# The first product of a chained matmul kernel in another order: high-by-high products first, then those with low parts

## The reference

```
x = x + einsum('bct,bcd->bdt', x, W0[cond0])        # 64 x 64 mixers of the rows
x = x + einsum('bct,bcd->bdt', x, W1[cond1])
x = x + x @ W.T + (x @ lora_A[i]) @ lora_B.T * 0.5   # 1024 x 1024, low rank 32
x = x + x @ W3[adapter].T                            # one of 8 matrices a batch
```

## Time and profile before

| | us |
|---|---|
| median of 3 runs | 394.82 |
| lowest and highest | 394.56, 395.0 |
| the profiled execution | 394.66 |
| its span, first to last instruction | 392.9 |

### The profile page before, as it was taken

The page is one execution under the profiler, slowest core; times in us unless marked ns, Lnnn a source line. Parts: engine busy times, 40 slices in busy tenths (PEclk is TensorE's granted clock), DMA queues, the critical chain, the costliest instruction groups (busy, mean ns, idle before and its releaser), DMA issues.

```text
span 392.9 us, 7604 instructions
## 1 busy us (share of the span) xinstructions
PE 380.2 (97%) x1736; PEld 316.4 (81%) x1736; DVE 268.3 (68%) x285; ACT 231.2 (59%) x307; POOL 123.3 (31%) x163
## 2 busy tenths in 40 slices
PE   8999999999999999999999999899999999999990
PEld 8888888888888888888888887688888888888860
DVE  4746967865855958547967439953699546899563
ACT  3798859387232775244483549554677357777361
POOL 0000340100003000024865427763258434576400
PEclk9999999999999999999999999999999999999996
DMA  7984902740348475406526224742276322762223
GB/s 225 396 313 158 375 3 79 261 180 19 107 173 288 182 277 166 180 21 214 175 93 221 58 55 123 260 133 55 56 235 211 97 57 56 270 219 54 56 58 88
DMA packets 24219, 61.37 MB, mean 156 GB/s; under 512 B 1938, under 2 KB 2066, under 8 KB 24146
## 3 DMA queue, kind: packets, MB, share of 16 engines
q1 hardware_dynamic: 23808, 60.30, 46.1%
q10 hardware_dynamic: 338, 0.24, 0.2%
HBM read 52.15 MB, written 8.39 MB: 154 GB/s over the span
## 4 chain that ended last, share of the span: by engine, by line
PE 96%; issue 1%; DVE 1%; ACT 0%; POOL 0%; ACTq 0%; DVEq 0%; POOLq 0%
PE ps L1400 44%; PE ps L1286 13%; PE ps L1287 13%; PE ps L1288 13%; PE ps L1427 4%; PE ps L1313 4%; PE ps L1325 2%; PE ps L1257 1%; PE ps L1265 1%; DVE stage L1236 0%; DVE stage L1177 0%; ACT stage L706 0%; DVE aT L1214 0%; PE ps L1446 0%; ACT stage L798 0%
## 5 line engine op out<-in xcount | busy, mean ns | idle before, releaser
L1400 PE MATMUL ps<-ring,aT 128*128 x784 | 180.8, 389 | 0.0
L1400 PEld LDWEIGHTS ps<-ring,aT 128*128 128x128 f32 x784 | 147.1, 188 | 30.8 <-issue 0.4
L1286 PE MATMUL ps<-ring 128*128 128x512 f32 x224 | 88.3, 394 | 0.0
L1287 PE MATMUL ps<-ring 128*128 128x512 f32 x224 | 88.0, 393 | 0.0
L1288 PE MATMUL ps<-ring 128*128 128x512 f32 x224 | 87.9, 392 | 0.0
L429 POOL TENSOR_TENSOR aT<-xT,aT 128x512 fp32r<-128x512 f32 (+1 forms) x36 | 56.3, 1585 | 51.3 <-ACT aT L685 45.2
L1149 DVE TENSOR_TENSOR ring<-raw,ring 128x1024 f32 (+1 forms) x40 | 63.8, 1655 | 5.1 <-ACT ring L671 5.0
L694 ACT ACTIVATE aT<-ps 64x1024 fp32r<-64x1024 f32 x32 | 32.7, 1021 | 48.1 <-PE ps L1400 47.6
L1177 DVE TENSOR_TENSOR stage<-ps,stage 64x1024 f32<-64x1024 f32 x30 | 36.7, 1222 | 26.3 <-ACT stage L706 25.7
L1166 DVE TENSOR_TENSOR aT<-ps,aT 64x1024 fp32r<-64x1024 f32 x32 | 39.1, 1222 | 22.6 <-ACT aT L694 21.9
L1288 PEld LDWEIGHTS ps<-ring 128*128 128x128 f32 x224 | 42.6, 190 | 9.0
(11 more groups left out here) (82 smaller groups left out, 314.5 us busy)
## 6 DMA issues: line engine op xcount, KB each, us to landing
raw<-w3t SPq DMA_DIRECT2D x40, 512.0 KB, 4.4
ring_f<-xt SPq DMA_DIRECT2D x8, 1024.0 KB, 7.7
raw<-xt SPq DMA_DIRECT2D x8, 1024.0 KB, 5.1
out<-stage SPq DMA_DIRECT2D x30, 256.0 KB, 3.0
ring_f<-wt SPq DMA_DIRECT2D x4, 1024.0 KB, 7.4
xT<-xt SPq DMA_DIRECT2D x3, 1024.0 KB, 9.5
xT<-wt SPq DMA_DIRECT2D x2, 1024.0 KB, 15.2
ring_f<-xt SPq DMA_DIRECT2D x4, 256.0 KB, 6.4
```

Source lines behind the costliest of these rows:

```text
L1286: pe.matmul(dst, hi_of(qw)[:, k, cs], hi_of(qx)[:, k, :], start=start and k == 0, stop=False, skip_group_check=True)
L1287: pe.matmul(dst, hi_of(qw)[:, k, cs], lo_of(qx)[:, k, :], start=False, stop=False, skip_group_check=True)
L1400: last = pe.matmul(acc(i)[:, n, :], x3_split(i, k, start, P), ring[:, bass.ds(off + (part * D + n * 512), 512)], start=(k == 0 and j == 0) ...
```

## The change

Four things are done:

1. SP issues W's tile ahead of x's tile, for each `k`.
2. ACT takes W's tile before x's. For `k` = 0, columns 128 to 511 of W, which the identity doesn't touch, are rounded as soon as the tile has landed (new semaphore `w_hi_off`), then x's tile, then W's first 128 columns after `A11`. For `k` = 1 to 3 it waits for `A11`, makes `w_hi`, then `x_hi`.
3. PE takes, for each `k`, the four high-by-high matmuls (one to each bank; for `k` = 0 in the order `o` = 1, 2, 3, 0), then the four with `x_lo`, then the four with `w_lo`. Each group of four waits for just its parts.
4. The events that tell of a finished bank are then on the last four matmuls of the product.

DVE's order is unchanged. The count of matmuls is unchanged (48).

```diff
@@ SP
             for k in range(HALF):
                 one = slice(k, k + 1)
+                sp.dma_start(raw_of(w_slot(0))[:, one, :], w_block(1, 1)[:, one, :]).then_inc(s(f"w_in0_{k}"), 16)
                 sp.dma_start(raw_of(x_slot(0))[:, one, :], x_block(1, 0)[:, one, :]).then_inc(s(f"x_in0_{k}"), 16)
-                sp.dma_start(raw_of(w_slot(0))[:, one, :], w_block(1, 1)[:, one, :]).then_inc(s(f"w_in0_{k}"), 16)
@@ ACT
-            for k in range(HALF):
+            act.wait_ge(s("w_in0_0"), 16)
+            act.activation(hi_of(w_slot(0))[:, 0, P:], raw_of(w_slot(0))[:, 0, P:], ACT.Copy).then_inc(s("w_hi_off"), 1)
+            act.wait_ge(s("x_in0_0"), 16)
+            x_hi(0, raw_of(x_slot(0)), slice(0, 1))
+            act.wait_ge(s("A11"), 1)
+            act.activation(hi_of(w_slot(0))[:, 0, 0:P], raw_of(w_slot(0))[:, 0, 0:P], ACT.Copy).then_inc(s("w_hi"), 1)
+            for k in range(1, HALF):
                 one = slice(k, k + 1)
+                act.wait_ge(s("A11"), k + 1)
+                w_hi(0, raw_of(w_slot(0)), one)
                 act.wait_ge(s(f"x_in0_{k}"), 16)
                 x_hi(0, raw_of(x_slot(0)), one)
-                act.wait_ge(s("A11"), k + 1)
-                w_hi(0, raw_of(w_slot(0)), one)
@@ PE
+            w, x = (hi_of(w_slot(0)), lo_of(w_slot(0))), (hi_of(x_slot(0)), lo_of(x_slot(0)))
             for k in range(HALF):
-                for o in range(HALF):
-                    last = main(0, 0, ps_l2(0, 0, o), o, True, True, (k,))
-                    if k == HALF - 1:
-                        last.then_inc(s("l2"), 1)
+                for a, b in ((0, 0), (0, 1), (1, 0)):
+                    high = (a, b) == (0, 0)
+                    if high and k == 0:
+                        pe.wait_ge(s("w_hi_off"), 1)
+                        pe.wait_ge(s("x_hi"), 1)
+                    elif high:
+                        pe.wait_ge(s("w_hi"), k + 1)
+                        pe.wait_ge(s("x_hi"), k + 1)
+                    elif b:
+                        pe.wait_ge(s("x_lo"), k + 1)
+                    else:
+                        pe.wait_ge(s("w_lo"), k + 1)
+                    for o in (1, 2, 3, 0) if high and k == 0 else range(HALF):
+                        if high and k == 0 and o == 0:
+                            pe.wait_ge(s("w_hi"), 1)
+                        last = pe.matmul(ps_l2(0, 0, o), w[a][:, k, P * o:P * (o + 1)], x[b][:, k, :],
+                                         start=high and k == 0, stop=k == HALF - 1 and a == 1, skip_group_check=True)
+                        if k == HALF - 1 and a:
+                            last.then_inc(s("l2"), 1)
```

More of the change, by code:

```diff
@@ L1281, in main @@
                     if whole_wait:
-                        whole = 1 if w == 0 and n == 0 else 2
-                        pe.wait_ge(s("w_lo"), HALF * w + (k // whole + 1) * whole)
-                        pe.wait_ge(s("x_lo"), HALF * n + (k // whole + 1) * whole)
+                        pe.wait_ge(s("w_lo"), HALF * w + (k // 2 + 1) * 2)
+                        pe.wait_ge(s("x_lo"), HALF * n + (k // 2 + 1) * 2)
                     cs = slice(P * o, P * (o + 1))
```

## The result

The changed kernel takes 396.21 us (median of 9 runs, 395.24 to 397.52) against 394.37 us of the kernel before (9 runs, 393.38 to 395.0). The ratio is 1.005, with a 95% interval of 1.0034 to 1.0066: slower by 1.3 to 2.6 us. The profiled execution took 396.93 us with a span of 395.2.

What follows compares the result with a forecast made beforehand. PE was taken to bound the kernel, holding 96% of the chain of waits. The median 394.82 us, plus 0 on PE (from -0.16) and 0 to 0.2 of stall, gave 394.9, own range 394.5 to 395.1, wider range 394.3 to 395.6.

Steps and rivals of the forecast that it cites:

- Worth 0: Head of the first product: PE arrives at 9.53, after low parts (9.06) and high parts (8.0), so its change gains 0.
- a sign that the forecast is wrong: PE's first 23 us: any idling of PE there would show the forecast wrong.
- The line of identity, high parts, low parts: Tiles 1 to 3 on ACT and DVE: steps run one after another, 2.75 us a tile; mixers' copy starts at 16.28.
- DVE's `a_tab` part would end at 22.19, as ACT reaches the selection at 22.24, so it adds nothing: Ahead of the first selection: waiting for `a_tab` adds 0 to ACT's lateness of 0.6 us, or 0.8 without overlap.
- The room at the first delta: `low_split` was done at 36.52, weights loaded at 37.26: room of 0.74 us before lateness of ACT stalls PE.
- the second place: Second low-rank products: x block 3 done at 48.27, weights loaded at 49.05, so 0.78 us of room.
- Rival 1: ACT and DVE steps don't overlap: ACT 1.9 us late, PE stalls at the first delta, 396.1 us; chance 0.09 in full.
- Rival 2: Head of the first product: PE did wait there unseen, and the new order gains, giving 394.5 us; chance 0.09.
- Rival 3: First product: the clock changes level at another moment; chance 0.03 for a gain, 0.02 for a loss.
- 392.6: Gain case of Rival 3: clock rises at the product's start, eleven matmuls run faster, 2.2 us gained; chance 0.03.
- 402 us: Loss case of Rival 3: alternating banks keep the clock low to the product's end, 7.2 us lost; chance 0.02.

Runs made afterwards that it cites:

- pe_only: The kernel before with only PE's new order (first four high-by-high products wait for all of `w_hi` of tile 0): 394.16 us, ratio 0.9993.
- act_only: The kernel before with only ACT's and SP's part of the change, PE keeping its old order: 395.99 us, ratio to before 1.0039.
- regs_after: The changed kernel with ACT reading the eight labels of the first four selections into registers early: 394.35 us, ratio to before 0.9992.
- regs_before: The kernel before with eight labels read early, four ahead of the first tile and four behind the mixers' copy: 394.5 us, ratio 0.9998.
- delay_one: The kernel before with one more ACT copy between x block 2 and the first selection: 394.45 us, ratio 1.0.
- delay3: The kernel before with three more ACT copies between x block 2 and the first selection: 397.72 us, ratio 1.0083.
- pool_b: The kernel before with PE's new order, early label reads, `b_split` and `b_diff` copies on GpSimd, DVE's part of them earlier: 394.76 us, ratio 1.0013.

## Why the prediction was wrong, point by point

- **PE's part, right in the sum and wrong in its reason.** "Worth 0" holds: `pe_only` is at 0.9993. But not because PE comes late to the product's head. I read from one profile that PE begins at 9.53 with the low parts long ready. In all eleven other profiles with the warm-up the mixer products take 2 to 2.6 us instead of 3.68, and end between 7.4 and 8.5, before the low parts are ready. There the new order does start the product earlier: at 8.53, against 9.90 in `act_only`, which has the same order on ACT and SP. The wait is also shorter (1.08 us against 2.02), the level held after it, and PE reaches the next product at 20.06 against 23.77. This lead goes into the waits up to the first delta, because `low_split` comes no earlier (38.59 against 38.71). PE idled ahead of 8.53 and again ahead of 20.06, in the first 23 us, which I had named as a sign that the forecast is wrong.
- **The line of identity, high parts, low parts: right.** 2.75 us for a tile were forecast and 2.72 measured; the mixers' copy was to start at 16.28 and started at 16.55, x block 2 at 20.33 and 20.58. The late landing of x's first tile (ACT starts on it at 7.75, where 7.38 was forecast) covers that difference of 0.25.
- **"DVE's `a_tab` part would end at 22.19, as ACT reaches the selection at 22.24, so it adds nothing": the step that failed.** The two times were nearly right (22.45 and 22.59), the conclusion wasn't. Ahead of a selection stands not only ACT but its sequencer, and that waits for `a_tab` first and reads labels then. I had compared the wait with the end of ACT's work, where it had to be compared with the start of the sequencer's reading ahead, 1.3 us before. It cost 0.85 + 0.38 = 1.23 us of the 2.08 in the changed kernel's profile. Without it ACT would have been 0.85 us late, 0.1 beyond the room that I had read. `regs_after` took it away, together with reads that had cost time before as well, and had the loss gone.
- **The room at the first delta, right as a place, not fixed as a room.** 0.74 us was the room of one execution, the one in which the level rose late. By it a lateness of 2.08 gives 1.3 of stall, and the weights were loaded 1.40 later. The two profiles with the old order on PE, the level up at the mixer products and ACT on time (`regs_before`, `delay_one`) load them at 36.62 and 36.66, PE being the later one in both; against those the changed kernel loads 2.0 later. The medians say 1.8 (1.3 to 2.6). At the second place, the second low-rank products, PE didn't wait (weights loaded at 50.36 against 49.05), as the rival had it for a PE that is late itself.
- **Rival 1 came true in size, not in cause.** It gave 396.1 for a lateness of 1.9, by steps that don't overlap. They do overlap; 1.23 us of the lateness of 2.08 came from the register reads. I had given it 0.09, and the range ended below it.
- **Rival 2** had the right event and a wrong worth: with the old order PE does wait at the head where the level is up early (2.02 us in `act_only`, 1.79 in `regs_before`), and removing that wait moved the time by nothing measurable. **Rival 3** (the bank order and the clock): in the changed kernel's profile the level was up before the product, the event of its first half, but the 392.6 did not come, because the gain ended in the waits up to the first delta. The 402 us did not come either; they were the price of the lower level held to the product's end, and 48 matmuls that change the bank each time ran at 0.233 us. A level that falls and rises would have cost less than that.
- The changed kernel's span is 2.3 us longer, 1.4 of it up to the first delta. At the adapters' first product the distance is 1.3 (188.2 against 186.9), at their last 1.8. The rest lies in stages that the change doesn't touch, and is within what the fourteen profiles differ by there; I put it to no cause.

## What to carry to other kernels

Room on a path has to be read from several executions, or worked out for both orders of arrival: here the one profile showed a rise of the clock that came late, which none of the eleven others with the same warm-up had. When a wait stands ahead of work whose address comes from a register, the thing that gets late is the sequencer's reading ahead, not the engine's next instruction; read such registers before the wait. And an engine that is made faster ahead of a common meeting point gains nothing that can be measured while the other chain into that point is the later one, as PE's new order alone showed.

## What the runs showed of the hardware

- **TensorE's level at the start differs between executions.** In the profile before, the mixer products took 3.68 us and matmuls of 512 columns were 0.43 us apart until about 14 us; in eleven other profiles with the same warm-up the mixer products took 2 to 2.6. The granted clock in the profile's rows stood at 1.00 in both (from 5.92 to 14.5 us in the kernel before), so it can't be used for this first rise; the distance of starts can.
- **It can fall back after a short pause.** In `regs_before` the mixer products ran fast, PE then waited 1.79 us, and the product began at the lower level, 0.43 us a matmul for the first six. This fall the granted clock does show: 0.50 from 9.70 to 12.30.

```profile
5.90 2.00 PE L1275 MATMUL ps<-stage 64*128 64x64 f32 x32
9.70 0.79 PE L1296 MATMUL ps<-ring 128*128 128x512 f32 x1 [1.79 <-DVE ring L841]
10.29 0.63 PE L1297 MATMUL ps<-ring 128*128 128x512 f32 x1
10.71 0.63 PE L1298 MATMUL ps<-ring 128*128 128x512 f32 x1
```

  The same came after pauses of 2.02 us in `act_only` and 1.38 in `delay_one` (granted clock 0.50 again). After 1.08 us in the changed kernel, 0.83 in `regs_after` and 0.67 in `delay3` the level held. In `pool_b` the pause was 0.89, and the level fell: 0.57 from 8.7 to 12 us, and 12.77 us for the 48 matmuls.
- **A register read on ACT's sequencer** takes 0.28 us (the first one 0.48) and its arithmetic 0.15; with the rest a selection costs 0.64, more than the 0.52 from one copy to the next where the registers were read before (`regs_after`).
